# Slots of the first layer in a new order, gates through Tanh, and fp32r products of the summed activations

## The reference, cut to what matters

```
x = x + 0.5 * L0_ffn(layernorm(x))      # top 2 of 8 experts, low-rank
x = x + L0_attn(layernorm(x))           # gated scan and a small MLP
x = x + 0.5 * L0_ffn(layernorm(x))
x = x + 0.5 * L1_ffn(layernorm(x))      # top 1 of 8 experts, d 128, f 512
x = x + L1_attn(layernorm(x))
x = x + 0.5 * L1_ffn(layernorm(x))
```

```
h1 = t@w1.T + 2*(t@a1[e].T)@b1[e].T     # h3 likewise with w3, a3, b3
act_e = silu(h1)*h3
out = sum_e w_e * (act_e@w2.T + 2*(act_e@a2[e].T)@b2[e].T)
```

## Time and profile before

| | |
|---|---|
| median of 3 runs | 1057.73 us (1056.75 to 1062.28) |
| profiled execution, its own time | 1054.69 us |
| its span | 1053.0 us |
| mean granted TensorE clock | 0.992 |
| PE matmul busy | 980.6 us (93%) |
| DVE, ACT, POOL busy | 711.2, 507.9, 500.1 us |
| fp32r matmuls, lines 362 to 364 | 416 each |

### The profile page before, as it was taken

How to read it: one execution, slowest core, us unless ns; L and a number is a source line. 1 busy time by engine, 2 the same in 40 slices (tenths; PEclk the granted TensorE clock), 3 DMA queues, 4 the chain that set the end, 5 groups by cost and what they waited for, 6 DMA issues and landing times. The chain is left out here.

```text
span 1053.0 us, 15574 instructions
## 1 busy us (share of the span) xinstructions
PE 980.6 (93%) x4429; PEld 669.9 (64%) x4429; DVE 711.2 (68%) x2140; ACT 507.9 (48%) x1039; POOL 500.1 (47%) x485
## 2 busy tenths in 40 slices
PE   3999999999999999999999999899988999889993
PEld 2766667656565665656566656477864667648873
DVE  5787779788786877879797776445543667634542
ACT  3433454655646556564453332144534777515451
POOL 3456555554535545354654655524451155423443
PEclk9999999999999999999999999999999999989997
DMA  6069000000000000000000002146534000015651
GB/s 181 1 284 415 3 1 1 1 1 1 1 0 2 0 1 1 1 0 1 12 3 9 11 11 71 39 137 197 166 94 140 1 22 22 22 42 178 194 174 34
DMA packets 42900, 65.12 MB, mean 62 GB/s; under 512 B 7153, under 2 KB 25121, under 8 KB 40640
## 3 DMA queue, kind: packets, MB, share of 16 engines
q1 hardware_dynamic: 37824, 55.59, 16.1%
q0 software_dynamic: 4992, 8.54, 2.4%
HBM read 37.20 MB, written 28.74 MB: 63 GB/s over the span
## 5 line engine op out<-in xcount | busy, mean ns | idle before, releaser
L362 PE MATMUL bank<-split 128*128 128x512 f32 x416 | 206.9, 497 | 7.8 <-DVE ud L1267 4.1
L364 PE MATMUL bank<-split 128*128 128x512 f32 x416 | 165.2, 397 | 0.0
L363 PE MATMUL bank<-split 128*128 128x512 f32 x416 | 164.8, 396 | 0.0
L863 ACT ACTIVATE sil<-bank 128x512 f32<-128x512 f32 x128 | 76.2, 595 | 116.0 <-PE bank L364 115.2
L1644 POOL TENSOR_TENSOR gsum<-act 128x512 f32<-128x512 f32 x64 | 84.9, 1327 | 81.5 <-DVE act L1203 81.4
L421 PE MATMUL bank<-act,a 128*128 128x512 f32 x256 | 117.6, 592 | 0.0
L362 PEld LDWEIGHTS bank<-split 128*128 128x128 f32 x416 | 79.5, 191 | 48.8 <-issue 17.4
L1199 DVE TENSOR_TENSOR act<-bank,sil 128x512 f32<-128x512 f32 x128 | 87.8, 686 | 17.2 <-PE bank L364 14.2
L363 PEld LDWEIGHTS bank<-split 128*128 128x128 f32 x416 | 79.9, 192 | 28.3 <-issue 18.6
L688 PE MATMUL bank<-xlT,e 128*128 128x256 f32 x368 | 91.2, 392 | 5.1 <-ACT xlT L1068 2.7
L1203 DVE TENSOR_TENSOR act<-act,wT 128x512 f32<-128x512 f32 x128 | 91.7, 716 | 4.4
(11 more groups left out here) (283 smaller groups left out, 1957.6 us busy)
## 6 DMA issues: line engine op xcount, KB each, us to landing
e<-e_dram SPq DMA_DIRECT2D x92, 256.0 KB, 3.1
rows_in<-yw SPq DMA_DIRECT2D x17, 1056.0 KB, 17.8
xin<-rows_in SPq DMA_DIRECT2D x46, 132.0 KB, 3.0
x<-rows_out SPq DMA_DIRECT2D x8, 256.0 KB, 4.7
rows_in<-yw,slot_i POOLq DMA_INDIRECT x64, 2.3
rows_out<-ob,ids POOLq DMA_INDIRECT x46, 2.3
out<-ob,ids POOLq DMA_INDIRECT x46, 2.4
act<-b_dram SPq DMA_DIRECT2D x2, 256.0 KB, 3.1
```

Of the source, the lines that this page charges most:

```text
L362: mm(dst, w[0], m[0], start=start, stop=False, **more)
L363: mm(dst, w[0], m[1], start=False, stop=False, **more)
L364: return mm(dst, w[1], m[0], start=False, stop=stop, **more)
L863: af(sil[(k - 1) % 2][:, :], bank[BH1[STEPS[k - 1][0] % 2]][:, :], ACT.Silu).then_inc(silu_done.sem, 1)
```

## The change

- PE's `value(1, ...)` becomes `value_sum`: a2 times the **sum** of both experts' activations, in fp32r (12 matmuls). The first values are then masked by the difference of the masks, and POOL's `values` subtracts.
- `down` is in fp32r too (12 matmuls in four calls). The sum is written in place (`act1[j]`) and split once: ACT's `sums_high` rounds it, POOL's `sums_low` subtracts. `down(g, 0)` and `down(g, 1)` stay in the slot; `down(l, 2)` and `down(l, 3)` run in the next slot. w2 and a2 are split once, in slot 0.
- Gates: Tanh with scale 0.5 and half the bias, then a Copy with 0.5 and 0.5; each behind its own product.
- Order on PE: `pre_T` after `h(1, 1)`; `logits` after `h(1, 2)`; the masks, `up` and the gate products earlier and spread out; `value` last.
- Order on DVE: `f_norm` moves from the head of a slot to the end of the slot before, behind `act(8)` and `a_leaky(1)`; `masked` goes ahead of `act(7)` and `act(8)`; `a_scans` before `first_values`.
- On ACT and POOL the calls follow this order. The indirect DMAs of `r_scatter` go to the head of the next slot, behind `low`, up to slot 16.
- `h2T` and the `a_up` products use bank `BV`, the routing's transposes `BSIDE`. Buffers share memory in another way; weights of the second layer are loaded after the last `h(3, 8)`.

The diff, cut to its core (PE, then DVE, then POOL and ACT):

```diff
+                def value_sum():
+                    if l is None:
+                        return
+                    pe.wait_ge(*r_done(l, 1))
+                    pe.wait_ge(*sum_low(l))
...
+                    for j in range(J):
+                        last = mm3(bank[BV][:, :], tuple(w[:, rows(j)] for w in a2s), gs[j], j == 0, j == J - 1)
+                    last.then_inc(v_ready.sem, 1)
...
-                    pe.wait_ge(*summed(g, j + 1))
-                    mm(bank[BOUT][:, :], w2[:, j, :], gsum[j % 2][:, :], start=j == 0, stop=False).then_inc(w2_used.sem, 1)
+                    pe.wait_ge(*sum_low(n, j + 1))
+                    mm3(bank[BOUT][:, :], tuple(w[:, rows(j)] for w in w2s), gs[j], j == 0, False)
...
-                h(1, 1); h(3, 1)
+                h(1, 1)
+                pre_T()
+                h(3, 1)
                 a_T()
                 h(1, 2)
+                logits()
...
+                down(l, 2)
+                h(3, 2)
                 a_den()
-                h(3, 2)
-                pre_T()
+                down(l, 3)
+                value_sum()
                 a_back()
-                value(1, range(J))
...
+                a_gate(2)
                 h(3, 8)
-                value(0, (0, 1))
-                a_gate(0)
...
+                value((0, 1))
                 a_gate(3)
+                value((2, 3))
```

New on ACT and POOL:

```diff
+                def sums_high(n, j):
...
+                    act.wait_ge(*summed(n, j + 1))
+                    act.wait_ge(*v_ready(n - 1))
+                    af(gs[j][0], act1[j][:, :], ACT.Copy).then_inc(sum_high.sem, 1)
...
-                        af(dst[:, :], bank[BSIDE][:, :], ACT.Sigmoid, bias=bias).then_inc(gates_saved.sem, 1)
+                    af(dst[:, :], bank[BSIDE][:, :], ACT.Tanh, bias=half[:, i:i + 1], scale=0.5).then_inc(gates_saved.sem, 1)
+                    act.wait_ge(*gates_saved(n, i + 1))
+                    af(dst[:, :], dst[:, :], ACT.Copy, scale=0.5, bias=0.5).then_inc(gates_done.sem, 1)
...
+                def sums_low(n, j):
...
+                    pool.wait_ge(*sum_high(n, j + 1))
+                    pool.tensor_tensor(out=gs[j][1], in0=act1[j][:, :], in1=gs[j][0].bitcast(F32), op=ALU.subtract).then_inc(sum_low.sem, 1)
```

More of the change, by code:

```diff
@@ L407, in h, with value @@
                         mm3(b[:, :], cut(lora), uds[p][i], False, True, skip_group_check=True).then_inc(ready.sem, 1)
-                def value(e, js):
-                    n = g if e == 0 else l
+                def value(js):
+                    if g is None:
+                        return
+                    if js[0] == 0:
+                        pe.wait_ge(*r_done(g - 1))
+                        if s.a_up is not None:
+                            pe.wait_ge(*m_saved(s.a_up))
+                    for j in js:
+                        pe.wait_ge(*weighted(g, STEP[j, 0]))
+                        last = mm(bank[BV][:, :], a2[:, j, :], act0[j][:, :], start=j == 0, stop=j == J - 1)
+                    if js[-1] == J - 1:
+                        last.then_inc(v_ready.sem, 1)
@@ L411, in value, with down @@
+                def down(n, j):
                     if n is None:
                         return
[L413 to L421, removed]
@@ L994, in a_T @@
                             af(w[:, :], wif[:, k:k + 1].to_broadcast([P, P]), ACT.Copy).then_inc(spread.sem, 1)
+                        af(half[:, 0:2], bif[:, :], ACT.Copy, scale=0.5).then_inc(spread.sem, 1)
+                        af(half[:, 2:3], vecs[:, 5:6], ACT.Copy, scale=0.5).then_inc(spread.sem, 1)
+                        act.wait_ge(spread.sem, 4)
                     act.wait_ge(*ynT_a(n))
@@ L1363, in a_scans @@
                     v.tensor_tensor_scan(num[:, :], gf[:, :], iv[:, :], 0.0, ALU.mult, ALU.add).then_inc(scan_steps.sem, 1)
-                f_norm()
                 r_factors(s.r_pre)
                 act(1)
+                split_low(LOW_DVE[:2])
+                top2(0)
+                act(2)
                 a_den()
-                act(2)
+                top2(1)
+                split_low(LOW_DVE[2:])
+                second_values()
                 a_mix()
-                second_values()
                 r_read(s.r_sort, BSIDE)
@@ L1375, in first_layer @@
                 r_top1(s.r_sort)
-                split_low(LOW_DVE[:2])
-                top2(0)
+                act(4)
                 a_add()
-                act(4)
-                top2(1)
-                split_low(LOW_DVE[2:])
+                f_stats()
+                act(5)
                 f_add()
-                act(5)
-                f_stats()
+                a_stats()
                 act(6)
-                a_stats()
                 r_stats(s.r_stat, xf_done, NCH)
                 a_leaky(0)
+                masked(0)
                 act(7)
+                masked(1)
+                act(8)
                 a_leaky(1)
+                f_norm()
                 r_rows(s.r_sort, BSIDE)
-                masked(0)
-                act(8)
                 a_leaky(2)
-                masked(1)
+                a_scans()
                 first_values()
-                a_scans()
             def r_stats(n, updated, first):
```

291 lines of the change are left out of this document (166 added, 125 removed).

## The result

| | before | after |
|---|---|---|
| median | 1060.01 us (1056.75 to 1062.53) | 1109.39 us (1108.04 to 1112.44) |
| ratio, 95% interval | | 1.0472 (1.0429 to 1.0514) |
| span of the profiled execution | 1053.0 us | 1110.7 us |
| mean granted TensorE clock | 0.992 | 0.969 |

The forecast was 1050 us, with a range up to 1064. The change lost 49 us.

What follows compares the result with a forecast made beforehand. PE was taken as the first layer's bound: 24.3 us of work and 8.7 of waits go, 21.1 of new waits and 4.1 of small terms come, so 7.8 less: 1046.9 profiled, 1050 us median, range 1032 to 1064.

Steps and rivals of the forecast that it cites:

- The bound: First layer: PE bounds the kernel, busy 44.41 of 44.9 us in a full gate slot, with a few waits.
- 24.3 us of PE work: Value and down products as fp32r matmuls over 16 slots: 10.7, 8.2 and 5.4 us saved.
- The 8.7 us of old waits: PE's three largest waits, on DVE's second masked input 4.1, ACT's gates 3.6, denominators 1.0: all counted as gone.
- What is late next: Slot ends: f_norm, moved behind act(8) beside POOL's stream, takes 4.2 us, bounds 1.11 and 5.45; pre_T waits for it.
- The Copies: Three more copies on ACT in gate slots, set against table loads of 1283 ns that go: costed at nothing.
- The split of the sums: Four ACT roundings and four POOL subtractions per slot, some 5 us on POOL: taken as covered, costed at nothing.
- The late loads: Loads moved behind the last h(3, 8): claimed hidden by the end of the routing.
- New waits: 21.1 us, at 14 slot ends: PE's waits for DVE's late results at slot ends: 9.0, 1.2, 0.7, 6.0 and 4.2 us by kind of slot.
- the prediction's groups: Slot ends sorted by gates and leaky steps: 1.8, 0.6, 0.7, 1.5 or 2.1 us of wait each.
- every two-operand DVE instruction waits too: Slot ends: act multiply, leaky steps and scan also wait for POOL, 26.6 us more, 1077 us; chance 0.12.
- its point of 2.4: Mean new wait in us at the 14 slot ends past which the change is slower by 0.5%, instead of 1.5.
- 4.1: Small terms: slot 0's pre_T 1.0, a_out 1.0, slots 12 to 15 1.0, end of slot 15 1.1 us.

Runs made afterwards that it cites:

- kernel 12: kernel 5 with one move alone, PE's down(l, 2) behind h(3, 2): 1064.36 us, 1.0047 of the kernel before.
- kernel 11: The changed kernel in its own order, POOL's total and up_low on 8 of 512 columns from the third chunk on: 1041.26 us, 0.9828.
- kernel 6: kernel 5 with down and summed value products in plain fp32 of the high parts only, low parts left out: 1085.29 us, 1.0234.
- kernel 5: The changed kernel with DVE's f_norm right behind act(7) and both leaky steps ahead of act(8), around masked(1): 1069.11 us, 1.0074.
- kernel 10: The kernel before with its gates alone as Tanh and a Copy, in their old places: 1060.43 us, 1.0024.
- kernel 3: The changed kernel with twelve unused bf16 matmuls on PE ahead of pre_T's wait for f_norm, from chunk 2 on: 1100.93 us, 1.0393.
- kernels 8: The kernel before with pre_T alone moved early, behind h(1, 1) on PE and silu(1) on ACT: 1126.51 us, 1.0619.

## Why the prediction was wrong

**What held.** The bound, the place and the mechanism. Against 24.3 us of PE work forecast, PE is busy for 18.4 us less than before in kernel 12 and for 23.3 less in kernel 11, both with the changed kernel's products; in time they are worth 16.2 by kernel 6. So the saving was sized about right; how much of the distance to 24.3 is an over-sized term is not shown. The matmuls of lines 373 to 375 are 544 each, 128 more than before. The 8.7 us of old waits went but for 2.1 for `ud`. What is late next is `f_norm`, behind POOL's stream, at 14 slot ends, as forecast. The Copies cost nothing that the runs show. The split of the sums, costed at nothing, cost 6.0 us of waits for its low parts here, and 21.4 in kernel 5. The late loads were not tried by themselves.

**The step that failed** is the sum "New waits: 21.1 us, at 14 slot ends". It is 47.0 (44.8 for `yn_f`, 2.2 for `iv`). By slot ends, in the prediction's groups: 17.1 for 9.0 (slots 5 to 9), 3.5 for 1.2 (3 and 4), 3.3 for 0.7 (10), 13.8 for 6.0 (0, 1, 2 and 13), 9.4 for 4.2 (11 and 12). In the slot of the rows above it is 3.8 us (3.34 + 0.43) for the forecast 1.8, in the other four of its group 3.3. Term by term in that slot:

| term of the sum | forecast | measured |
|---|---|---|
| act(8) | 1.33 | 2.20 (399.39 - 397.19) |
| first leaky step | 0.6 | 1.68 (401.07 - 399.39) |
| `f_norm` | 4.2 | 4.91 (405.98 - 401.07) |
| second leaky step | 0.6 | 0.60 |
| scan | 1.55 | 1.13 |

In this slot three quarters of the excess (0.87 + 1.08 of 2.66, before the scan gives 0.42 back) are instructions that were priced from rows where POOL was idle; the rest is `f_norm`, which lasts 4.9 to 5.4 us at every slot end for the 4.2 taken, inside its bound of 5.45. The first is the rival "every two-operand DVE instruction waits too", given 0.12. Its mechanism came, and the mean wait, 3.4 us, is past its point of 2.4. That its sum of waits, 21.1 + 26.6 = 47.7 us, is what was measured (47.0) is in part luck: by its prices a slot end of the first group would be 4.3 us (3.3 to 3.8 measured) and one of the last 3.4 (4.7 measured). Against it the prediction had held one row, the scan that took "its" 1.62 us beside POOL. That was misread. With POOL idle the same scan takes 1.21 us (six of the eight in the changed kernel, all eight in kernel 11), so 1.62 was already 0.4 us too long; under the whole stream it takes 2.31 in the changed kernel and 2.29 in kernel 5. The row spoke for the rival. The Trainium skill's rule on two SBUF inputs (SBUF — State Buffer, "Who interferes with whom") had been read as if POOL alone were the late one; by that rule either engine can be the one that waits, and the traces agree: 1.55 and 1.76 us on DVE, 1.73 and 1.75 on POOL.

**The term that was missing** is the clock. The rival's time was 1077, on the profiled execution 18.8 us more than before; 57.7 were measured. Of the 38.9 us between, idle time that no case held gives 12.4 (55.5 more in the stretch, where 47.7 + 4.1 - 8.7 = 43.1 was summed): among it 4.2 for ACT's `wak`, below, which kernel 10 has too, in the old order, and 6.0 for the low parts of the sums (POOL, line 1701, from the start on). PE's busy time gives 24.3: it didn't fall at all, where the sum had taken 24.3 off it. 18.4 of this (kernel 12) to 23.3 (kernel 11) are the saving that those kernels show and the changed kernel hides behind a slower clock; the 1 to 5.9 left are open. The rest, 2.1, lies outside the stretch. So 18 to 23 us are clock, an estimate by the difference of kernels with nearly the same matmuls (2812, and 2808 in kernel 12); kernel 3 bounds it from below by a run, 8.5. In this kernel one us of clock came on every two and a half to three of new idle time (18.4 to 23.3 for 55.5).

**What stays open.** Whether more can be had from this order than kernel 12 gives. From the first Silu of a slot to that of the next, its slots 0 to 2 are longer than before (30.6, 34.8 and 36.8 us for 29.5, 32.2 and 32.3), and the stretch from the last chunk's product to the experts is 104.6 us for 92.3; of that second excess 4.2 is the wait for `wak`, 2.6 are two waits for the low parts of the last sums, and the granted clock is 0.95 there for 1.00; the rest was not tried.

## What to carry over

When an instruction is moved beside a stream of GpSimd, price it and every two-operand neighbour on VectorE by rows taken beside such a stream (here 1.6 to 1.8 us for 0.7, and 5.0 for 1.1), or look for GpSimd's own idle stretch and put it there: for `f_norm` and the leaky steps that alone was worth 40 us. And ask of a row used as the undisturbed price whether GpSimd was idle in it: the scan's 1.62 us wasn't one. A new wait of TensorE can cost more than its length, since the granted clock may fall behind it. And where an order brings a consumer forward, the whole chain of producers has to come with it; taking one wait away only shows the next one in the queue.

## What the runs showed unasked

A wait of about 1.2 us of TensorE was followed by 7 us at the lower clock in one slot and by none in another; fillers in the waits made the kernel 8.5 us faster.

And a stall of DVE and ACT together, for which no engine's work accounts. Rows of the timelines of DVE and ACT in kernel 5:

```profile
687.93 0.19 DVE L1509 TENSOR_TENSOR pos<-bank,nxt 128x32 f32<-128x32 f32 x1 [5.76 <-remote]
688.01 0.28 ACT L870 ACTIVATE wak<-bank 128x128 f32<-128x128 f32 x1 [6.38 <-remote]
```

PE had ended the products for both by 684.2; PE then waits 4.2 us for `wak`. The profile of the kernel before has no such stall at this place; all the thirteen others have it (4.0 to 4.3 us), among them those of kernels 8 and 10, which have none of the late loads and none of the new products. So it doesn't come from them; where it comes from was not settled. The profiled execution before is also 5.3 us faster than the median of its kernel: most executions of it may have the stall, which no run here shows.
